# Top-32 attention masks moved off VectorE: eight of ten to GpSimd in one pass, two to ScalarE

## The reference

```
scores = q k^T * scale             # 3136 x 3136 per head
vals, idx = top_k(scores, 32)      # per query row
out = softmax(vals) @ v[idx]
```

## Time and profile before

| | us |
|---|---|
| median of 3 runs | 40168.95 |
| lowest, highest | 40162.17, 40170.39 |
| the profiled execution, its time | 40166.83 |
| the profiled execution, its span | 40165.2 |
| VectorE busy | 34028.5 (85%) |
| TensorE busy | 27334.3 (68%) |
| GpSimd busy | 23707.4 (59%) |
| ScalarE busy | 21387.4 (53%) |
| TensorE clock granted | 0.801 of full |

### The profile page before, as it was taken

One profiled execution on the slowest core, in us unless ns is written; L12 is line 12 of the kernel. 1 busy time (PEld: TensorE's weight loads), 2 busy tenths in 40 slices (PEclk: granted clock), 3 DMA queues, 4 the chain that ended last, 5 costly groups with the idle time before them and its releaser, 6 DMA issues. The chain is left out here.

```text
span 40165.2 us, 616606 instructions
## 1 busy us (share of the span) xinstructions
PE 27334.3 (68%) x190808; PEld 12487.9 (31%) x190809; DVE 34028.5 (85%) x144824; ACT 21387.4 (53%) x28193; POOL 23707.4 (59%) x9390
## 2 busy tenths in 40 slices
PE   4557676666767667767347677777776777674399
PEld 4533332222333323333123233333332333331122
DVE  5659999999999999999669999999999999996611
ACT  1126665555666656656146566666665666663111
POOL 0017776666867667867037677777776777773000
PEclk7778888888888888888578788888888888886555
DMA  0010000000000000000110000000000000001100
GB/s 36 8 51 5 5 5 5 4 4 4 5 5 5 5 4 5 5 5 5 51 50 5 4 5 5 5 5 5 5 5 4 5 5 5 4 5 42 55 10 6
DMA packets 133141, 454.41 MB, mean 11 GB/s; under 512 B 29244, under 2 KB 85444, under 8 KB 111240
## 3 DMA queue, kind: packets, MB, share of 16 engines
q1 hardware_dynamic: 129256, 410.72, 3.0%
HBM read 244.71 MB, written 165.93 MB: 10 GB/s over the span
## 5 line engine op out<-in xcount | busy, mean ns | idle before, releaser
L225 POOL TENSOR_SCALAR B<-S,M 128x3136 bf16<-128x3136 f32 (+1 forms) x1920 | 15768.6, 8213 | 7934.6 <-DVE M L525 7848.3
L493 DVE MAX8 C<-S 128x8 f32<-128x112 f32 x89600 | 18738.3, 263 | 1002.3 <-issue 751.5
L418 ACT COPY S<-banks 128x896 f32<-128x896 f32 (+1 forms) x12800 | 10210.9, 815 | 8585.1 <-DVE C L493 3667.1
L439 ACT ACTIVATE W<-banks 128x1024 f32<-128x1024 f32 (+1 forms) x9524 | 9735.7, 1023 | 2747.3 <-PE banks L333 2696.0
L324 PE MATMUL banks<-Q,K 99*128 99x512 bf16 (+2 forms) x22550 | 6836.4, 390 | 3341.2 <-ACT S L418 2742.3
L286 PE MATMUL banks<-K,Q 96*128 96x448 bf16 x22400 | 6852.1, 385 | 3128.3 <-ACT S L418 2747.0
L230 POOL CAST Z<-B 128x3136 fp8e4<-128x3136 bf16 (+1 forms) x1920 | 6704.5, 3492 | 380.9 <-PE banks L333 136.4
L333 PEld LDWEIGHTS banks<-NEG,Z 128*128 128x128 fp8e4 (+1 forms) x80450 | 5968.7, 105 | 2753.9 <-issue 823.1
L333 PE MATMUL banks<-NEG,Z 128*128 128x128 bf16 (+3 forms) x80450 | 6817.7, 230 | 0.0
L369 PE MATMUL banks<-W,V 128*32 128x512 f32 (+1 forms) x45100 | 6726.3, 577 | 109.2 <-ACT W L442 79.0
L535 DVE TENSOR_SCALAR Z<-S,M 128x3136 fp8e4<-128x3136 f32 x1280 | 6033.2, 4713 | 369.7 <-PE banks L333 369.6
(11 more groups left out here) (200 smaller groups left out, 21899.3 us busy)
## 6 DMA issues: line engine op xcount, KB each, us to landing
q<-ln_o SPq DMA_DIRECT2D x20, 1568.0 KB, 5.1
ln_x<-y SPq DMA_DIRECT2D x16, 1568.0 KB, 6.0
K<-k_parts SPq DMA_DIRECT2D x130, 147.0 KB
Q<-q_parts SPq DMA_DIRECT2D x130, 147.0 KB
q_parts<-pj_parts SPq DMA_DIRECT2D x24, 784.0 KB, 4.7
k_parts<-pj_parts SPq DMA_DIRECT2D x24, 784.0 KB, 7.8
V<-v_rows SPq DMA_DIRECT2D x130, 112.5 KB, 7.4
v_rows<-pj_vt SPq DMA_DIRECT2D x8, 1800.0 KB, 11.2
```

What stands on the lines that cost most here:

```text
L225: chained(lambda: pool.tensor_scalar(m.B[0:rows, :], m.S[0:rows, slot(tile), :], m.M8[0:rows, side(i), t, 31:32], None, ALU.is_lt))
L418: act.copy(m.S[0:rows, slot(tile), at:at + CW * w].rearrange("p (a n) -> p a n", a=w), m.AB[0:rows, pair(score_at[a]):pair(score_at[a]) + ...
L439: ins = act.activation(m.W[:, e % 4, 0:n_banks, :], m.AB[:, b:b + n_banks, :], ACT.Exp)
L493: ins = dve.max(m.C[0:rows, tile % 2, TOP_AT + k:RANKED:CHUNKS], m.S[0:rows, slot(tile), CHUNK * k:CHUNK * k + CHUNK])
```

## The change

GpSimd's two instructions for a mask become one with two operations, (score < threshold) x 56, written as unsigned bytes into `Z`. The byte 56 is the bit pattern of 1.0 in the eight-bit float that TensorE reads. The buffer `B` and the waits around it are gone; the wait for a free mask slot now stands ahead of the comparison. The mask slots are shared out anew: "DPPDPDPPDP" becomes "PPAPPPPAPP". Of ten masks VectorE makes none (before 4), GpSimd 8 (before 6), ScalarE 2, by max(0, threshold - score) into the new bfloat16 buffer `ZA`. ScalarE's mask for tile t stands in its queue behind the last copy of tile t + 3.

```
-MAKERS = "DPPDPDPPDP"
+MAKERS = "PPAPPPPAPP"
+ONE = 56.0
+BEHIND = 3
...
 # GpSimd, mask(tile)
                 pool.wait_ge(found, tile + 1)
-                masks_done = sum(maker(x) == "P" for x in range(tile))
-                if masks_done:
-                    pool.wait_ge(z_pool, masks_done)
-                chained(lambda: pool.tensor_scalar(m.B[0:rows, :], m.S[0:rows, slot(tile), :],
-                                                   m.M8[0:rows, side(i), t, 31:32], None, ALU.is_lt))
                 if mask_freed(tile):
                     pool.wait_ge(e_mm, mask_freed(tile))
-                pool.wait_ge(part, parts[0])
-                pool.tensor_copy(mask_at(tile)[0:rows, :], m.B[0:rows, :], saturate=False).then_inc(z_pool, 1)
+                pool.tensor_scalar(mask_at(tile)[0:rows, :].bitcast(U8), m.S[0:rows, slot(tile), :],
+                                   m.M8[0:rows, side(i), t, 31:32], ONE, ALU.is_lt, ALU.mult).then_inc(z_pool, 1)
...
 # ScalarE
+            def mask(tile):
+                i, t = divmod(tile, NT)
+                rows = tile_rows(t)
+                act.wait_ge(found, tile + 1)
+                if mask_freed(tile):
+                    act.wait_ge(e_mm, mask_freed(tile))
+                act.activation(mask_at(tile)[0:rows, :], m.S[0:rows, slot(tile), :], ACT.Relu,
+                               bias=m.M8[0:rows, side(i), t, 31:32], scale=-1.0).then_inc(z_act, 1)
...
                 if kind == "score":
                     keep(x)
+                    if x % AP == AP - 1 and x >= AP * BEHIND and maker(x // AP - BEHIND) == "A":
+                        mask(x // AP - BEHIND)
                     continue
...
+            for tile in range(max(TILES - BEHIND, 0), TILES):
+                if maker(tile) == "A":
+                    mask(tile)
...
 # buffers
-("B", [128, TOK], BF16)
+("ZA", [128, MAKERS.count("A"), TOK], BF16)
```

More of the change, by code:

```diff
@@ L7 @@
 FP8 = mybir.dt.float8e4
+U8 = mybir.dt.uint8
 I32 = mybir.dt.int32
@@ L608, in attend_memory @@
             ("Q", [128, 2, TOK], BF16), ("K", [128, 2, TOK], BF16), ("V9", [128, NT * (HD + 1)], F32),
-            ("V1", [128, 2, NT, 32], F32), ("S", [128, RING, TOK], F32), ("Z", [128, MASKS - MAKERS.count("A"), TOK], FP8),
-            ("B", [128, TOK], BF16), ("W", [128, 4, 2, QW], F32), ("O4", [128, QW], F32), ("OS", [HD + 1, 2, QW], F32),
+            ("V1", [128, 2, NT, 32], F32), ("S", [128, RING, TOK], F32), ("Z", [128, MASKS - MAKERS.count("A"), TOK], FP8), ("ZA", [128, MAKERS.count("A"), TOK], BF16),
+            ("W", [128, 4, 2, QW], F32), ("O4", [128, QW], F32), ("OS", [HD + 1, 2, QW], F32),
             ("C", [128, 2, RANKED], F32), ("C8", [128, NT], F32), ("M8", [128, 2, NT, 32], F32),
@@ L623, in _ @@
             def _(pool):
-                for t in (m.V1, m.Q, m.K, m.Z, m.M8, m.VI):
+                for t in (m.V1, m.Q, m.K, m.Z, m.ZA, m.M8, m.VI):
                     pool.memset(t[:], 0.0).then_inc(zeroed, 1)
@@ L644, in _ @@
             def _(dve):
-                dve.wait_ge(zeroed, 6)
+                dve.wait_ge(zeroed, 7)
                 dve.memset(m.K[MAX_AT:MAX_AT + 3, :, :], 1.0)
```

## The result

| | before | after |
|---|---|---|
| median, us | 40170.39 (7 runs) | 40312.19 (7 runs) |
| lowest, highest | 40162.17, 40178.25 | 40304.47, 40313.26 |
| ratio to before | | 1.0035, 95% interval 1.0023 to 1.0047 |
| span of the profiled execution | 40165.2 | 40310.6 |

The account below looks back on a forecast made before the run. VectorE was taken as the bound, at 226.7 us a clean head. Outside the blocks 8554.8, plus 127.4 heads of 192, plus searches 2553.5 gave 35569 us; forecast's own range 34040 to 36970, whole range 33700 to 39700.

Parts of the forecast that it names:

- part 2: GpSimd's queue: 20 one-pass masks a head at 8.21 us plus 14.4 us of small work, 178.6 us a head.
- the pass costs more and GpSimd becomes the bound: GpSimd: a second operation makes a mask 10.9 us, a head 232.4, searches half hidden; 39440 us; chance 0.21.
- Part 1: VectorE: its ten masks a head and their slot waits go, from 226.7 to a floor of 176.7 us.
- Part 3: ScalarE: five masks a head at 2.90 us, 14.5 us together, 171.5 busy; alone no bound, threshold already there.
- The chain's upper end of 196.1 us: TensorE and ScalarE in one chain: at most 181.6 us a head plus 14.5 for ScalarE's masks.
- The rival's sum: Outside the blocks 8554.8, plus 127.4 heads of 232.4, plus 1277 for searches half hidden behind GpSimd's backlog: 39440 us.
- The gate of 9.5 us: Mask-slot wait at tiles 5 to 7: three masks and `shift_parts`, 26.2 us, fit in 29.9; not at 9.5 a mask.
- The moved wait: ScalarE's mask holds copies and exponentials, or slot waits bind: 210 to 225 us a head, 37900 to 39800; chance 0.07.
- The lock in the searches: VectorE's search instructions L568 and L570 may block behind a running GpSimd one, at most 1.4 ms.
- No change: Whole kernel: the change does nothing, VectorE's floor being misread; chance 0.01.
- dearer pass: GpSimd's single pass takes 10.9 us a mask and GpSimd becomes the bound: 39440 us, chance 0.21.
- slower: GpSimd: both operations at the comparison's price, 16.4 us a mask, 342.4 a head, 52180 us; chance 0.17.

## Why the prediction was wrong

**The step that failed is the price of the single pass** in part 2. The lower end, 8.21 us, was taken, with the reason that conversion at the output need not add a pass. That reason was right (the one-operation kernel) but not to the point: the second operation adds 2.65 us. The rival "the pass costs more and GpSimd becomes the bound" priced it at 10.9 us, measured 10.86, and with chance 0.21 stood behind the forecast. That it came so near was luck: it took 2.7 us from the length of a cast, and what is added is a second operation, not a cast.

**Part 1 held.** VectorE's masks cost what the rows said, for the reason given, and tiles without one keep their pace of 6.70 us where nothing holds VectorE up. No kernel ran at the floor of 176.7 us; the kernel with all masks on VectorE gives 231 - 9.8 - 25 x 1.84 = 175.2 for it.

**Part 3 held.** ScalarE's mask: 2.92 for 2.90 us, no wait for the threshold. The chain's upper end of 196.1 us was not exceeded with two masks of ten: 187.7 us.

**The sum with its own price of the pass** was tested by the one-operation kernel: 35569 us forecast, 35352 measured. Terms cancel in this: a head takes 187.7 us and not 192 (-548), searches with what the blocks' ends change take 26690 - 127.4 x 187.7 = 2777 and not 2553.5 (+224), and outside the blocks it is 35346.3 - 26690 = 8656 against 40165.2 - 31612 = 8553 (+103).

**The rival's sum** gave 39440 us, and the kernel takes 870 us more, beyond the range's upper end too. The terms, from the windows:

| term | reckoned | measured | us |
|---|---|---|---|
| clean head, x 127.4 | 232.4 | 229.1 | -420 |
| blocks shorter than their clean heads, the first head above all (28780 against 127.4 x 229.1) | 0 | -407 | -407 |
| 99 searches | 12.9 each | 26.1 each | +1307 |
| outside the blocks (40310.6 - 31364 against 40165.2 - 31612) | 0 | +393 | +393 |

39440 - 420 - 407 + 1307 + 393 = 40313. The rows of -407 and +393 are nearly one thing, booked twice: the windows are cut at VectorE's thresholds, and GpSimd's backlog, built up in a block's first head, is worked off after its last threshold. So with the rival's own price of a pass the change still brings nothing because of one cost that the rival took as half hidden, the searches.

*Searches.* I had them half behind GpSimd's backlog. They come back as idle time of GpSimd. Its masks in the changed kernel, then in the one without searches:

```profile
L227 POOL TENSOR_SCALAR Z<-S,M 128x3136 uint8<-128x3136 f32 (+1 forms) x2560 | 27776.2, 10858 | 3040.0 <-PE banks L331 1566.8 <-DVE M L537 1389.8
```

```profile
L227 POOL TENSOR_SCALAR Z<-S,M 128x3136 uint8<-128x3136 f32 (+1 forms) x2560 | 27775.1, 10858 | 487.1 <-DVE M L537 302.0 <-PE banks L331 100.3
```

The idle time grows by 2553 us, nearly all of the 2584: waits for a threshold (L537) by 1088 us, waits for a free mask slot (L331) by 1467. The timeline of GpSimd around two searches in a row in the changed kernel shows both:

```profile
9429.67 10.85 POOL L227 TENSOR_SCALAR Z<-S,M 128x3136 uint8<-128x3136 f32 x1
...
9442.25 10.87 POOL L227 TENSOR_SCALAR Z<-S,M 128x3136 uint8<-128x3136 f32 x1
9471.77 10.85 POOL L227 TENSOR_SCALAR Z<-S,M 128x3136 uint8<-128x3136 f32 x1 [18.65 <-DVE M L537]
...
9550.33 10.85 POOL L227 TENSOR_SCALAR Z<-S,M 128x3136 uint8<-128x3136 f32 x1 [29.14 <-PE banks L331]
```

And that of VectorE in the same stretch:

```profile
9442.33 3.42 DVE L575 MATCH_REPLACE8 S<-M,S 128x3136 f32<-128x3136 f32 x1
...
9471.44 0.24 DVE L537 MAX8 M<-C 128x8 f32<-128x92 f32 x1
```

The search writes scores and mask of its tile anew, so it waits for the group's masks (`masks_made` in `check`) and begins at 9442.2, just as GpSimd is through with them; over all searches VectorE sat idle 1398 us ahead of L575, where ahead of L563 before it was 265. By then the backlog is nearly used up: GpSimd makes one more mask and sits idle for 18.65 us until VectorE has its next threshold. VectorE's spare time lies ahead of the search, where it buys nothing.

The wait of 29.14 us is of the other sort. It ends 14 us after the next search, of which the last instruction ended at 9536. While VectorE searches it frees no slot of `S`, ScalarE can't copy scores, and the value works, which free the mask slots, stand behind these in the same list: ScalarE waits 2113.7 us for VectorE in this way, 67 times, up to 87.7 us. So the standstill reaches GpSimd once more, by way of TensorE. That the 26.1 us aren't hidden is shown by the kernel without searches, and the two sorts of idle time are measured; that this order of waits is their cause is read from the trace and the code and wasn't tried.

*Between blocks.* The window from the last threshold of the first block to the first of the second, in the changed kernel and then in the kernel before:

```profile
4858.00:4920.00 62.00, 13.43 (x72) 6.37 (x71) 10.70 (x64) 11.95 (x16) 41.92 (x17) 0.53 0.01 2
```

```profile
4859.00:4891.00 32.00, 12.09 (x71) 5.51 (x71) 10.41 (x62) 11.39 (x15) 12.71 (x12) 0.58 0.01 4
```

GpSimd is now behind VectorE when a block ends and works off its masks while all others wait: 41.9 us busy against 12.7, and the gap is 30 us longer. Its last mask starts 30.5 us after the last threshold; before, it was 0.6 us. Over all 15 gaps it is 356 us, 7 to 30 each. The next block's thresholds don't begin before these masks are done. Against this stand the first heads of 207 to 209 us: GpSimd begins a block without backlog, so the thresholds can come faster than its masks for one head. The two rows of the table sum to -14 us: together they cost nothing.

**The gate of 9.5 us.** I had three masks and `shift_parts` within 28 works as the place where it gets tight, and the waits of L302 for L245 are at that place. But it added nothing of its own: a clean head is GpSimd's sum, 217.2 + 11.9 us, and in the kernel without searches GpSimd waits for a mask slot only 16 times, 100 us in all. A queue that is full all the time has the slot it needs when it gets there.

**The moved wait** did not come up on ScalarE: its masks show no idle time in front. **The lock in the searches** was not put to the test: L580, the search's mask (L568 before), keeps its mean of 1853 ns, but neither it nor L582 behind it (L570 before) ever overlapped one of GpSimd's masks, in any of the 99 searches.

**"No change" got a chance of 0.01**, since I saw no mechanism for it. There was one, the bound moving to a queue nearly as long as the old one, for which chances should have been given between "dearer pass" and "slower" by the pass's price: at 10.9 us the rival's head of 232.4 us was already over the clean 226.7 of before, and its whole gain of 730 us hung on the 1277 us of searches that it took as hidden.

## What to carry to other kernels

When work moves to another engine, reckon that engine's whole queue per period with the dearest plausible price of the new instruction form, and look at how the new period stands to the old one: here 229.1 against 226.7 us left nothing to gain. One instruction with two operations is not one pass at the price of one operation on GpSimd (10.86 against 8.21 us here); ask whether the second is needed at all (a mask needs only to be above zero). Rare serial work on an engine that has become idle on average is not hidden unless the engine behind it has a backlog at that very time, and its standstill can come back a second time through the buffers that other engines then free late. A window cut at one engine's events can book another engine's backlog as a gain inside and a loss outside; look at both together.

## What the runs showed of the hardware

GpSimd's `tensor_scalar` over 128 x 3136 floats takes 8.21 us with one operation, to bfloat16 or to bytes alike, and 10.85 to 10.86 with two, comparison and multiplication or subtraction and minimum. Its cast from bfloat16 takes 2.80 us when VectorE makes no masks, and up to 4.18 beside them. TensorE takes the byte 1 as an eight-bit float above zero: the result stays right with it, where the kernel with GpSimd's masks out of effect is 5.6% off. VectorE's `tensor_scalar` of the same size takes 1.84 us. It was stretched, up to 8.95 us, only where it overlapped a comparison or a cast of GpSimd: so it was for all 1230 of 1280 that took over 1.9 us.
